# Splitting the expert weights of two stages once, ahead of time, on one Trainium2 core

## The reference, cut to what matters

```
shared_out = einsum('nh,dh->nd', silu(x @ sw1.T) * (x @ sw3.T), sw2)       # every token, 1024 hidden units
H = gelu(einsum('nd,ehd->enh', x, rw1));  O = einsum('enh,edh->end', H, rw2) # 8 routed experts, top 2 per token
y = (shared_out + einsum('end,ne->nd', O, combine)) / 3
...
sel = argmax(softmax(gelu(y[:, -1] @ Wp1 + bp1) @ Wp2 + bp2))              # one of 8 experts per batch
h = gelu(y @ W1[sel] + b1[sel])                                            # 512 -> 1024
reasoned = h @ W2[sel] + b2[sel]                                           # 1024 -> 512
x = x + y + 0.3 * (reasoned @ Wo + bo)
```

## Time and profile before

| | us |
|---|---|
| median of three runs (lowest, highest) | 2918.16 (2914.73, 2922.99) |
| profiled execution: span, first to last instruction | 2914.5 |
| PE busy | 2574.8 (88%) |
| DVE busy | 1479.1 (51%) |
| ACT busy | 1200.6 (41%) |
| POOL busy | 724.8 (25%) |
| weight splits in `stage_ffn`: DVE, ACT | 354.1, 256.6 |
| weight splits in `stage_routed`: DVE, ACT | 176.6, 152.4 |

### The profile page before, as it was taken

One profiled execution on the slowest core, in us unless ns is written; L12 is line 12 of the kernel. 1 busy time (PEld: TensorE's weight loads), 2 busy tenths in 40 slices (PEclk: granted clock), 3 DMA queues, 4 the chain that ended last, 5 costly groups with the idle time before them and its releaser, 6 DMA issues. The chain is left out here.

```text
span 2914.5 us, 41950 instructions
## 1 busy us (share of the span) xinstructions
PE 2574.8 (88%) x12487; PEld 2061.8 (71%) x12487; DVE 1479.1 (51%) x1826; ACT 1200.6 (41%) x1773; POOL 724.8 (25%) x604
## 2 busy tenths in 40 slices
PE   6999999977787568888888886699997999999999
PEld 1788888866666456666666664599996888888876
DVE  4311111146666577777777774477664233333346
ACT  3111111146676455555555552466664222222223
POOL 0222222021222146555555554000000111111100
PEclk9999999989899889999999998799998999999999
DMA  6222222034634253335333531566664111111125
GB/s 246 33 63 51 51 51 43 14 120 121 195 109 130 88 172 121 123 122 177 118 122 120 176 121 65 205 231 224 232 237 163 37 29 33 33 29 29 29 76 169
DMA packets 136778, 328.58 MB, mean 113 GB/s; under 512 B 41762, under 2 KB 44258, under 8 KB 129056
## 3 DMA queue, kind: packets, MB, share of 16 engines
q1 hardware_dynamic: 113744, 258.70, 27.1%
q0 software_dynamic: 22992, 69.37, 8.1%
HBM read 425.67 MB, written 77.76 MB: 173 GB/s over the span
## 5 line engine op out<-in xcount | busy, mean ns | idle before, releaser
L1083 DVE TENSOR_TENSOR s_w_lo<-s_w_raw,s_w_hi 128x1024 fp32r<-128x1024 f32 x256 | 354.1, 1421 | 3.0 <-ACT s_w_hi L1041 3.0
L1041 ACT ACTIVATE s_w_hi<-s_w_raw 128x1024 fp32r<-128x1024 f32 x256 | 256.6, 1052 | 103.8 <-PE s_z_ps L88 72.3
L395 DVE TENSOR_TENSOR s_h<-s_sg,s_up 128x512 f32<-128x512 f32 x64 | 43.9, 687 | 395.7 <-ACT s_sg L290 395.6
L86 PE MATMUL s_g<-wx_hi,s_x_hi 128*128 128x512 f32 x512 | 206.7, 404 | 6.5 <-DVE s_x_lo L1604 4.0
L88 PE MATMUL s_g<-wx_hi,s_x_lo 128*128 128x512 f32 x512 | 201.8, 394 | 0.0
L87 PE MATMUL s_g<-wx_lo,s_x_hi 128*128 128x512 f32 x512 | 201.1, 393 | 0.0
L607 POOL DMA_INDIRECT s_x<-in_x_rows,s_idx x72 | 92.4, 1284 | 405.5 <-DMA s_idx<-mid_slot_token 387.0
L1338 DVE TENSOR_TENSOR s_w_lo<-s_w_raw,s_w_hi 128x1024 fp32r<-128x1024 f32 x128 | 150.9, 1221 | 68.1 <-ACT s_w_hi L1290 66.4
L290 ACT ACTIVATE s_sg<-s_gate 128x512 f32<-128x512 f32 x64 | 38.3, 599 | 291.2 <-PE s_up L88 291.2
L86 PE MATMUL s_z_ps<-s_w_hi,s_ht_hi 128*128 128x512 f32 x256 | 110.6, 432 | 50.8 <-DVE s_ht_lo L1099 47.4
L1505 POOL DMA_INDIRECT s_y<-mid_hash_out,s_rec x32 | 31.5, 985 | 488.2 <-DMA s_rec<-mid_rec 488.2
(11 more groups left out here) (305 smaller groups left out, 7296.8 us busy)
## 6 DMA issues: line engine op xcount, KB each, us to landing
s_w_raw<-in_rw SPq DMA_DIRECT2D x144, 512.0 KB
s_w_raw<-in_w SPq DMA_DIRECT2D x32, 2048.0 KB
s_w_raw<-in_w SPq DMA_DIRECT2D x64, 1024.0 KB
s_w_raw<-in_w1h SPq DMA_DIRECT2D x16, 2048.0 KB, 8.2
s_w_raw<-in_w2h SPq DMA_DIRECT2D x16, 2048.0 KB, 7.7
mid_routed<-s_o_sb SPq DMA_DIRECT2D x72, 256.0 KB, 3.1
s_b<-in_b SPq DMA_DIRECT2D x32, 512.0 KB
s_x_grp<-in_xt_groups POOLq DMA_DIRECT2D x8, 1024.0 KB, 5.7
```

Source lines behind the costliest of these rows:

```text
L86: pe.matmul(out, a_hi, w_hi, start=first, stop=False, skip_group_check=True)
L1041: act.activation(hi[:, c], raw[:, c], ACT.Copy).then_inc(S[name + "_hi"], 1)
L1083: dve.tensor_tensor(lo[:, c], raw[:, c], hi[:, c], ALU.subtract).then_inc(S[name + "_lo"], 1)
```

## The change

The weights of the feed-forward experts and of the routed experts are split once, in `stage_shared`, and stored as high and low parts in DRAM: per group of tiles one expert, in ten units of 128x1024 (two of the routed expert, four of W1, four of W2), 80 units in all. Each is a load of 512 KB, one copy on ACT, one subtraction on DVE and a store of 1 MB. ACT now issues the stage's loads of tokens and stores of results, since SP issues the units.

`stage_routed` and `stage_ffn` no longer split weights. They read the parts back into rings: four buffers in `stage_routed` (`NW2`), three buffers in `stage_ffn` (`NW`, W1 and W2 of an expert taking one each). Which buffer holds a tile's weights is known only at run time. It is computed in tables, and SP, ACT and PE read it from there into registers: SP in `stage_routed` for each load, ACT in `stage_ffn`, which now issues the weight loads, and PE in both stages, whose matmuls take their weights at an address from a register.

`stage_ffn` also changes otherwise: the bias rows are loaded only where the expert is new; the shifted copy is made as two transfers of 112 and 15 rows; record buffers are doubled; the receptance is taken one step later, stands between `turn_h(1)` and `txr`, and writes to the bank of `th_ps`; `x` and the shared result are loaded by steps of their own; all lists are unrolled by two. In `stage_shared` POOL reads the slot numbers from SBUF instead of loading them again.

The core of the diff:

```diff
+            def parts(e, last=False):
+                for j in range(NPART):
+                    sp.wait_ge(S["part_lo"], e * NPART + j + 1)
+                    store_part(e, j)
+                    if j + 2 < NPART:
+                        raw_part(e, j + 2)
...
+            def part_hi(g, j):
+                turn = g * (NPART // 2) + j // 2
+                act.wait_ge(S[f"part_in{j % 2}"], turn * 16 + 16)
+                wait_for(act, S[f"part_out{j % 2}"], turn * 16)
+                act.activation(part[j % 2][:, 0].bitcast(FP32R), w_raw[:, j % 2], ACT.Copy).then_inc(S["part_hi"], 1)
...
+            def part_lo(g, j):
+                dve.wait_ge(S["part_hi"], g * NPART + j + 1)
+                dve.tensor_tensor(part[j % 2][:, 1].bitcast(FP32R), w_raw[:, j % 2], part[j % 2][:, 0].bitcast(FP32R),
+                                  ALU.subtract).then_inc(S["part_lo"], 1)
...
-            def load_w(name, c):
+            def load_w(layer, used):
                 def stage(i, n, turn):
                     expert = sp.value_load(route[0:1, 0, bass.ds(i, 1)], min_val=0, max_val=ER - 1)
                     new = sp.value_load(route[0:1, 1, bass.ds(i, 1)], min_val=0, max_val=1)
-                    wait_apart(sp, S[name + "_lo"], i - 1)
-                    sp.dma_start(w_raw[:, n % 2, c], ins["rw"][expert, :, c],
-                                 cond=new > 0).then_inc(S[f"{name}_in{n % 2}"], 16)
+                    s = slot(sp, i)
+                    wait_apart(sp, S[used], i - NW2 + 1)
+                    sp.dma_start(w[:, bass.ds(s, 1), layer].bitcast(FP32),
+                                 d["rw"][bass.ds(expert, 1), :, layer].rearrange("o p s n -> p o s n"),
+                                 cond=new > 0).then_inc(S[f"w{layer + 1}_in{n}"], 16)
...
-            software_pipeline(sp, RT, [(0, load_idx), (2, load_w("w1", slice(0, W1))),
-                                       (3, load_w("w2", slice(W1, W1 + W2))), (4, load_wo), (7, store)], NI)
+            software_pipeline(sp, RT, [(0, load_idx), (0, load_w(0, "mm1")), (1, load_w(1, "mm2")), (4, load_wo),
+                                       (4, store)], NI)
...
-                sp.dma_start(prev[1:P], x1[0:P - 1]).then_inc(S["prev_in"], 16)
+                for p0, p1 in ((0, 112), (112, P - 1)):
+                    sp.dma_start(prev[p0 + 1:p1 + 1], x1[p0:p1]).then_inc(S["prev_in"], 16)
...
+            def load_w1(i, n, turn):
+                e, new, s = expert(act, i), is_new(act, i), slot(act, 0, i)
+                wait_for(act, S["mm2"], i - 1)
+                wait_apart(act, S["h_ps"], 2 * i - 1)
+                for k in range(2):
+                    act.dma_start(half[:, bass.ds(s, 1), 2 * k:2 * k + 2].bitcast(FP32), d["w"][bass.ds(2 * e, 1), :, 2 * k:2 * k + 2].rearrange("o p k s n -> p o k s n"),
+                                  cond=new).then_inc(S[f"w1_in{k}"], 16)
...
+            def find_weights(i, n, turn):
+                now["up"], now["down"] = slot(pe, 0, i), slot(pe, 1, i)
...
             software_pipeline(pe, NB, [
-                (1, up(0)), (2, turn(z, "z_add", tz_ps, "xr_lo", 1, "tz")), (1, up(1)), (1, turn_h(0)),
-                (2, times_wo), (1, turn_h(1)),
-                (3, turn(xr, "xr", tz_ps, "z_lo", -2, "txr")), (0, turn(y, "y", ty_ps, "y_lo", 0, "ty")),
-                (1, down), (3, receptance)])
+                (1, find_weights), (1, up(0)), (2, turn(z, "z_add", tz_ps, "xr_lo", 1, "tz")), (1, up(1)), (1, turn_h(0)),
+                (2, times_wo), (1, turn_h(1)), (4, receptance),
+                (3, turn(xr, "xr", tz_ps, "z_lo", -2, "txr")), (0, turn(y, "y", ty_ps, "y_lo", 0, "ty")), (1, down)], 2)
```

More of the change, by code:

```diff
@@ L215, in _, with raw_part, store_part @@
                 units(u2)
[L217 to L228, removed]
-            units(NU // 2 - 1)
-            software_pipeline(sp, G, [(0, but_first(load_x)), (1, store_o)])
-            sp.wait_ge(S["o_out"], 16 * NB)
+            sp.wait_ge(S["logits_t"], G - 1)
+            sp.dma_start(x_raw, ins["xt_groups"][0]).then_inc(S["xt_in"], 16)
+            units(NU // 2 - 1)
+            def raw_part(e, j):
+                name, k = PARTS[j]
+                src = ins["rw"][e, :, k * HS:(k + 1) * HS] if name == "rw" else ins[name][e, :, k]
+                sp.dma_start(w_raw[:, j % 2], src).then_inc(S[f"part_in{j % 2}"], 16)
+            def store_part(e, j):
+                name, k = PARTS[j]
+                dst = d["rw"][e, :, k] if name == "rw" else d["w"][e * 2 + (name == "w2"), :, k]
+                sp.dma_start(dst, part[j % 2]).then_inc(S[f"part_out{j % 2}"], 16)
+            def parts(e, last=False):
[4 more added lines that the diff above has]
+                        raw_part(e, j + 2)
+                    elif not last:
+                        raw_part(e + 1, j + 2 - NPART)
+            sp.wait_ge(S["w_lo"], NU)
+            raw_part(0, 0)
+            raw_part(0, 1)
+            with sp.Fori(0, ER - 1) as e:
+                parts(e)
+            parts(ER - 1, last=True)
+            for n in range(2):
+                sp.wait_ge(S[f"part_out{n}"], 16 * ER * NPART // 2)
         @block.gpsimd
@@ L308, in _ @@
             software_pipeline(act, G, [(1, chunks), (0, but_first(x_hi)), (1, o_out)])
+            for n in range(2):
+                act.wait_ge(S[f"o_out{n}"], 16 * NB // 2)
         @block.vector
@@ new lines, in load_w2 @@
+            def load_w2(i, n, turn):
+                e, new, s = expert(act, i), is_new(act, i), slot(act, 1, i)
+                if isinstance(i, int) and i == 0:
+                    act.wait_ge(S["y"], 1)
+                wait_apart(act, S["h_ps"], 2 * i)
+                for k in range(2):
+                    act.dma_start(half[:, bass.ds(s, 1), 2 * k:2 * k + 2].bitcast(FP32), d["w"][bass.ds(2 * e + 1, 1), :, 2 * k:2 * k + 2].rearrange("o p k s n -> p o k s n"),
+                                  cond=new).then_inc(S[f"w2_in{k}{n}"], 16)
@@ L1144, in _, with weights @@
+                (1, h_lo(0)), (2, x1_), (1, h_lo(1)), (3, part_lo(xr_lo, tz_ps, xr_hi, "xr_hi", "xr_lo")),
+                (0, part_lo(y_lo, ty_ps, y_hi, "y_hi", "y_lo"))], 2)
         @block.tensor
         def _(pe):
-            def up(n):
-                def stage(i):
-                    if n == 0:
+            now = {}
+            def weights(layer, part, k, c):
+                return half[:, bass.ds(now[layer], 1), k, part, c * D:(c + 1) * D].rearrange("p o n -> p (o n)")
+            def find_weights(i, n, turn):
+                now["up"], now["down"] = slot(pe, 0, i), slot(pe, 1, i)
@@ L1176, in turn, with down @@
                 return stage
-            def down(i):
+            def down(i, n, turn):
                 wait_for(pe, S["z_add"], i)
```

446 lines of the change are left out of this document (222 added, 224 removed).

## The result

The change makes the kernel slower: 2988.5 us, median of four runs (2976.9 to 2992.1), against 2916.9 us before, four runs too (2914.7 to 2923.0). The ratio is 1.024, with an interval of 1.021 to 1.026. The forecast was 2908 us with a range of 2860 to 2975.

The account below looks back on a forecast made before the run. Bounds were taken as PE in shared, SP's table reads in routed, the slow shifted copy's loop in ffn. Terms +4 + 108 + 2.5 - 125 = -10.5 us on a 2914.5 us span gave 2904, with 3.7 added 2908 us; range 2860 to 2975.

Parts of the forecast that it names:

- The shared stage: Shared stage: PE hides the 80 added units; +4 us, from -2 to +60.
- against 403 GB/s with full queues: Shared stage: units want 280 GB/s in their chunks, set against the 403 GB/s that full queues reach.
- the opposite bound: Shared stage: at the 256 GB/s of an ffn weight load, transfers take 580 us, 60 us too long.
- The rival of a stage bound by its transfers: Shared stage: units slower than their 5.6 us chunk stall ACT, DVE and PE; about +40, at most +60; chance 0.10.
- Routed: Routed stage: added table reads and address work on SP make a tile 6.7 us; +108 us, from +62 to +166.
- the 0.32 us per tile for addresses: Routed stage, SP: buffer address and one more register instruction ahead of each transfer, about 2 x 0.16 us per tile.
- Ffn: Ffn stage: quicker copy removes the loop's bound and PE comes next; -125 us, from -80 to -145.
- the 19.3 given as PE's minimum: Ffn stage: PE's products, transpositions and handovers take 19.3 us per batch, the lower end for the 19.8 forecast.
- the half microsecond that was added: Ffn stage: PE's two table reads per step cost 1.2 us, about half hidden, so +0.5 us per batch.
- -118 + 8: Ffn stage: 31 batches at 19.8 instead of 23.61 us give -118 us; two more expert weight loads add +8.
- which look like the load of the stage, are not what ends last: Ffn stage: weight splits on ACT and DVE, 256.6 and 354.1 us, do not bound it; the late `x1` does.
- Choose: Choose stage: about eight more small vector instructions with handovers; +2.5 us, from 0 to +5.

Follow-up runs that it names:

- no_scatter: The changed kernel without POOL's 64 scatters of token numbers and the waits for them; 2887.0 us, ratio 0.990 to the kernel before.
- reads2: The changed kernel with the ring slot read twice on SP for each of a routed tile's two weight loads; 3055.4 us, ratio 1.046 to the kernel before.
- prev_two: The kernel before with one edit, the shifted copy made as two transfers of 112 and 15 rows; 2898.7 us, ratio 0.993.
- late_zero: The changed kernel with POOL's 32 zero fills held back until 40 of the 80 units are done, scatters in place; 2967.2 us, ratio 1.016.

## Why the prediction was wrong

**The shared stage: wrong, and with it the sum.** The forecast was +4 (-2 to +60); it is +118. The step that failed is the sentence that set the units' demand "against 403 GB/s with full queues" and took the opposite bound from a load at 256 GB/s. Both rates are of stretches of large transfers. That POOL's scatters run during most of the stage stood in the trace of before and was left out of the sum. Beside them all queues together moved 161 to 196 GB/s, below even the 256 of the opposite bound, and `no_scatter` puts some 93 of the 118 us on the scatters: without them the stage lasts 637 us in place of 730. In the half without scatters the sum held: a unit every 5.5 us, the pace of PE's chunks, and PE full. The rival of a stage bound by its transfers had the right chain (a unit later than its chunk, ACT and DVE in their lists, then PE) and the wrong price, 40 where 118 came.

**Routed: right.** Tile 6.48 us against 6.7, stage +90.6 against +108 (62 to 166). A read costs 0.556 us by `reads2` where 0.58 was taken: two more are 80 of the 91 us, so the 0.32 us per tile for addresses were too much; about 0.15 are left for them. The clock of the stage fell to 0.86 without deciding anything: 144 more reads on SP lengthen it by 80 us (`reads2`), so SP is what ends last.

**Ffn: the size right, the reason half of it.** -150 against -125 (-80 to -145), just past the end. A steady batch takes 18.7 us, below even the 19.3 given as PE's minimum, so the table reads and register instructions did not cost the half microsecond that was added. The two changes of expert cost 23 us where 8 were forecast, which makes 19.2 on average. From the first `x1` to the last it is 142.6 us less than before, where -118 + 8 was forecast; ahead of the first it is 4 us more (+1) and behind the last 11 less (-16). But the prediction said that the splits, "which look like the load of the stage, are not what ends last", and took PE to be next. They were a second limit directly behind the first, 23.5 us against 23.8, which the sum of DVE's durations (17.4 us per batch) hid, because they were measured while POOL mostly waited; in `prev_two` the same work is 20.7 us. It made no error in the total, as the change removed both, and that is luck: a forecast of the copy alone by the same reasoning (`prev_two`, 700 to 740 us for the stage) missed by 62 us or more.

**Choose** +3.3 against +2.5, and nothing in the later stages. With the shared term as measured, the other terms as forecast would have given 3022 us.

## What to carry to other kernels

Work that is put "under" a busy engine has to be priced against everything that is transferred at that time, tiny transfers above all, and not by bandwidth: ask what the other queues send in that stretch, and whether the work sits in an in-order list ahead of something that the bound engine waits for. If a stage has two limits, the second is seen only when the first is taken away alone; durations measured under the first limit may be too short for it.

## What the runs showed of the hardware

Scatters of 128 numbers of four bytes cost the large transfers beside them far more than their bytes: 0.26 us per 5.4 KB packet without scatters (`no_scatter`), 0.42 with scatters and fills and 0.50 with scatters alone (`late_zero`), in the same stretch of the stage, although the scatters' own packets take 1.3% of the engines' time. A copy of 127 rows of 2 KB took 15.6 us from its issue to the step that waits for it and, as 112 and 15 rows, 3.4 us. One more table read on SP cost 0.556 us (`reads2`). DVE's subtraction of 128x1024 from SBUF took 1421 ns on average beside a POOL that mostly waited and 1850 beside one that computed, and POOL's 128x512 step 1291 ns beside a DVE without splits and 2158 beside one with them; DVE's `h_pre` from PSUM took 678 and 679 ns.
